# Row maxima over two PSUM banks at once, and one bank for dense outputs and softmax sums

## The reference

```python
xn = group_norm(x)                                   # 32 groups
qkv = einsum('oc,bcn->bon', qkv_w, xn); q, k, v = split(qkv)   # per head
m = softmax(einsum('bct,bcs->bts', q * scale, k * scale), axis=-1)
h = einsum('bts,bcs->bct', m, v)
x = einsum('oc,bcn->bon', proj_w, h) + proj_b + x
```

## Time and profile before

| | us |
|---|---|
| median of 3 runs | 2266.51 (2265.88 to 2267.82) |
| profiled execution, its time | 2263.78 |
| its span, first to last instruction | 2262.0 |
| PE busy | 2193.9 (97%) |
| POOL busy | 1788.2 (79%) |
| DVE busy | 1692.7 (75%) |
| ACT busy | 1274.0 (56%) |

### The profile page before, as it was taken

How to read it: one execution, slowest core, us unless ns; L and a number is a source line. 1 busy time by engine, 2 the same in 40 slices (tenths; PEclk the granted TensorE clock), 3 DMA queues, 4 the chain that set the end, 5 groups by cost and what they waited for, 6 DMA issues and landing times.

```text
span 2262.0 us, 41861 instructions
## 1 busy us (share of the span) xinstructions
PE 2193.9 (97%) x10552; PEld 1091.3 (48%) x10552; DVE 1692.7 (75%) x2896; ACT 1274.0 (56%) x2321; POOL 1788.2 (79%) x567
## 2 busy tenths in 40 slices
PE   5799999999999999999999999999999999999998
PEld 3355454545545455454544545445454544545442
DVE  3677787777877778777777878768777777877772
ACT  2355656566565555656555565655656556565554
POOL 2388878888887978878887888878878788788785
PEclk8799999999999999999999999999999999999999
DMA  4222233322333322233322333222333322433210
GB/s 118 57 69 49 53 95 76 95 43 56 72 75 96 68 68 53 57 95 94 89 40 63 81 76 94 62 61 55 71 94 76 79 45 51 93 76 76 52 43 20
DMA packets 208771, 157.53 MB, mean 70 GB/s; under 512 B 166528, under 2 KB 166784, under 8 KB 208512
## 3 DMA queue, kind: packets, MB, share of 16 engines
q1 hardware_dynamic: 208512, 154.48, 29.8%
HBM read 36.39 MB, written 16.78 MB: 24 GB/s over the span
## 4 chain that ended last, share of the span: by engine, by line
PE 89%; DVE 4%; issue 3%; SPq 1%; ACT 1%; DMA 1%; DVEq 1%; POOL 0%; ACTq 0%; POOLq 0%
PE ps_t L365 25%; PE ps_v L400 21%; PE ps_m L382 19%; PE ps_d L421 9%; PE ps_a L413 5%; PE ps_d L436 5%; PE ps_d L429 5%; SPq L254 1%; DVE raw_max L656 1%; DVE stage_ql L673 1%; DVE att L717 1%; ACT pt L582 1%; DVE rden L707 0%; DMA qs<-neg_max 0%; PE ps_m L421 0%
## 5 line engine op out<-in xcount | busy, mean ns | idle before, releaser
L656 DVE TENSOR_REDUCE raw_max<-ps_m 128x1 f32<-128x512 f32 x2048 | 1332.4, 684 | 444.1 <-PE ps_m L382 413.4
L582 ACT ACTIVATE pt<-ps_t 128x512 f32<-128x512 f32 x2048 | 1141.8, 596 | 919.3 <-PE ps_t L365 913.0
L828 POOL TENSOR_TENSOR acc<-acc,pt 128x2048 f32<-128x2048 f32 x317 | 1448.8, 4570 | 89.5 <-ACT pt L582 61.5
L382 PE MATMUL ps_m<-ks,qs 96*128 96x512 f32 x2048 | 988.0, 483 | 9.0 <-DVE raw_max L656 8.0
L365 PE MATMUL ps_t<-qs,ks 97*128 97x512 f32 x2048 | 879.0, 430 | 30.3 <-issue 13.1
L365 PEld LDWEIGHTS ps_t<-qs,ks 97*128 97x128 f32 x2048 | 389.6, 191 | 656.4 <-ACT pt L582 366.9
L828 POOL TENSOR_TENSOR acc<-pt 128x2048 f32<-128x2048 f32 x64 | 291.8, 4560 | 327.0 <-ACT pt L582 327.0
L400 PE MATMUL ps_v<-pt,v 128*32 128x512 f32 x4096 | 546.5, 606 | 0.0
L382 PEld LDWEIGHTS ps_m<-ks,qs 96*128 96x128 f32 x2048 | 393.0, 192 | 152.2 <-issue 62.7
L421 PE MATMUL ps_d<-xn,wq 128*128 128x512 f32 x500 | 262.7, 608 | 8.2 <-ACT xn L614 5.7
L400 PEld LDWEIGHTS ps_v<-pt,v 128*32 128x32 f32 x4096 | 80.7, 108 | 185.1 <-ACT pt L582 115.1
(11 more groups left out here) (46 smaller groups left out, 531.9 us busy)
## 6 DMA issues: line engine op xcount, KB each, us to landing
ks<-stage_kh SPq DMA_DIRECT2D x256, 128.0 KB, 2.5
qs<-stage_qh SPq DMA_DIRECT2D x256, 128.0 KB, 2.5
ks<-stage_kl SPq DMA_DIRECT2D x128, 128.0 KB, 2.5
qs<-stage_ql SPq DMA_DIRECT2D x128, 128.0 KB, 2.5
qs<-neg_max SPq DMA_DIRECT2D x1024, 0.5 KB, 2.0
xn<-x_dram SPq DMA_DIRECT2D x16, 512.0 KB, 4.0
res<-x_dram SPq DMA_DIRECT2D x16, 512.0 KB, 4.2
between<-res SPq DMA_DIRECT2D x32, 256.0 KB, 2.1
```

The lines of the kernel that those rows point to most:

```text
L382: pe.matmul(ps_m[max_bank(u)][:, :], qs[b][0:KROWS, h, c:c + P], ks[b][0:KROWS, h, kf * HALF:(kf + 1) * HALF], start=True, stop=True).then ...
L582: act.activation(pt[t % 4][:, h, :], ps_t[u % 2][:, :], ACT.Exp, scale=SCALE).then_inc(exp_done, 1)
L656: dve.tensor_reduce(raw_max[:, e % 2, t, kf:kf + 1], ps_m[max_bank(u)][:, :], AX.X, ALU.max)\
L828: pool.tensor_tensor(acc[hf][:, :, :], a[:, :, :], pt[t % 4][:, :, :], ALU.add).then_inc(pool_added, 1)
```

## The change

- The scores for the maxima go in pairs to two double banks `ps_m` of 1024 values. DVE waits for the second of a pair and takes the maximum over both banks by one negating instruction straight into `neg_max`. `raw_max`, the joining instruction (L664) and the semaphore `neg_done` are gone. PE waits for `max_done` once a pair.
- That takes four banks, so `ps_d` and `ps_a` become one bank `ps_x`. The order of its users in a half is new: output 0 (units 0 and 2), the sums (unit 7) and their divide, output 1 (11 and 13), output 2 (17 and 19), output 3 (23 and 25). Each waits for the readers of the one before. Group statistics move to unit 61, their additions to 50, ACT's normalisation to units 11, 15, 19, 23, and POOL's scale and shift behind its last addition.
- SP issues the row of head 3 before the next slot's staging, and interleaves that staging with rows as in later slots.

```diff
-DENSE_AT = 1
-SUMS_AT = 10
+DENSE_AT = ((0, 2), (11, 13), (17, 19), (23, 25))
+SUMS_AT = 7
 DIVIDE_AT = (1, 2, 2, 3)
-GN_AT = 51
-NORMALISE_AT = (13, 17, 25, 29)
+ADD_QUARTERS_AT = 50
+GN_AT = 61
+NORMALISE_AT = (11, 15, 19, 23)
...
-        ps_m = [bank(f"ps_m{b}") for b in range(MAX_BANKS)]
+        ps_m = [ctx.enter_context(nc.psum_tensor(f"ps_m{b}", [P, NH, HALF], F32)) for b in range(2)]
         ps_v = bank("ps_v")
-        ps_d = bank("ps_d")
-        ps_a = bank("ps_a")
+        ps_x = bank("ps_x")
...
-            for e in range(HG - 1):
+            for e in range(HG):
                 load_row(e, 0, e)
-            for h in range(HG):
-                stage_head(1, 1, h)
-            load_row(HG - 1, 0, HG - 1)
-            for u in range(ROWS_AT, UNITS, MAX_GROUP):
-                slot_row(plain(0), u)
...
+            def output_taken(s, hf, r, first, has_second):
+                if hf == 1 and has_second:
+                    pe.wait_ge(qkl_done, 4 * (s.n + 2) + r + 1)
+                elif hf == 0 and s.g == 0 and not first:
+                    pe.wait_ge(proj_done, 4 * (s.j - 1) + r + 1)
+                elif hf == 0 and s.g == 1 and has_second:
+                    pe.wait_ge(v_done, 4 * (s.j + 1) + r + 1)
...
+                if writes and part == 0:
+                    if r > 1:
+                        output_taken(s, hf, r - 1, first, has_second)
+                    elif r == 1:
+                        if not (first and hf == 0):
+                            pe.wait_ge(norm_done, NH * s.n + hf)
...
                     if u == SUMS_AT and not first:
-                        sums(prev, NH - 1, stats_done)
+                        bank_for_sums(s, 0, first, has_second)
+                        sums(prev, NH - 1)
...
-                dve.tensor_reduce(raw_max[:, e % 2, t, kf:kf + 1], ps_m[max_bank(u)][:, :], AX.X, ALU.max)\
-                   .then_inc(max_done, 1)
-                if w % MAX_GROUP == MAX_GROUP - 1:
...
+                dve.tensor_reduce(neg_max[:, e % HG, t:t + 1], ps_m[max_pair(u)][:, :, :].rearrange("p k s -> p (k s)"),
+                                  AX.X, ALU.max, negate=True).then_inc(max_done, 1)
```

More of the change, by code:

```diff
@@ L111, in row_at, with max_pair, dense_at @@
     return NT * slot_n + e
[L114 to L119, removed]
+def max_pair(u):
+    return u // NH % 2
+def dense_at(u, later=0):
+    for r, steps in enumerate(DENSE_AT):
+        if (u - later) % (UNITS // NH) in steps:
+            return r, steps.index((u - later) % (UNITS // NH))
+    return None, None
 def attention_layers(nc, x, w_qkv, w_proj, pars, bias_v, bias_proj, ident_in, group_in, out):
@@ L259, in load_row @@
                 hf, h = e // HG, e % HG
-                sp.wait_ge(neg_done, row + 1)
-                for t in range(NT // NH):
+                sp.wait_ge(max_done, ROW_TILES * (row + 1))
+                for t in range(ROW_TILES):
                     c = hf * HALF + t * P
@@ L332, in _ @@
             turn = B // 2 - 1
+            slot(plain(0))
             body(0, 0, 0)
@@ L376, in scores_for_max @@
                     pe.wait_ge(staged[h], 16 * STAGE_DMAS * (n + 1))
-                back = next(k for k in range(1, UNITS) if max_bank((u - k) % UNITS) == max_bank(u))
-                if not isinstance(n, int) or UNITS * n + w >= back:
-                    pe.wait_ge(max_done, UNITS * n + w - back + 1)
+                pair = UNITS // NH * n + w // NH
+                if kf == 0 and not (isinstance(pair, int) and pair < 2):
+                    pe.wait_ge(max_done, pair - 1)
                 c = hf * HALF + t * P
-                pe.matmul(ps_m[max_bank(u)][:, :], qs[b][0:KROWS, h, c:c + P],
-                          ks[b][0:KROWS, h, kf * HALF:(kf + 1) * HALF],
-                          start=True, stop=True).then_inc(sm_ready, 1)
+                mm = pe.matmul(ps_m[max_pair(u)][:, kf, :], qs[b][0:KROWS, h, c:c + P],
+                               ks[b][0:KROWS, h, kf * HALF:(kf + 1) * HALF], start=True, stop=True)
+                if kf == NH - 1:
+                    mm.then_inc(sm_ready, 1)
             def weighted_values(s, hf, t):
@@ L439, in project_out, with group_stats @@
                     mm.then_inc(proj_ready, 1)
-            def group_stats(j, nsums):
+            def group_stats(j):
                 pe.wait_ge(mv_summed, j + 1)
-                aux_free(nsums)
-                mm = pe.matmul(ps_a[:, 0:2 * CT], group[:, :], channel_mv[:, :, :], start=True, stop=True)
+                mm = pe.matmul(ps_x[:, 0:2 * CT], group[:, :], channel_mv[:, :, :], start=True, stop=True)
                 mm.then_inc(gm_ready, 1)
-            def dense(s, u, first, has_next, has_second):
[L450 to L473, removed]
-                    if part == 0:
[L475 to L486, removed]
@@ L499, in slot @@
-                stats_done = s.j + 2 if s.g == 0 and not first and has_third else None
                 for u in range(UNITS):
                     scores_t(s, u)
-                    if u % HG == DENSE_AT:
-                        dense(s, u, first, has_next, has_second)
+                    dense(s, u, first, has_next, has_second)
                     if has_next or AHEAD + u < UNITS:
```

143 lines of the change are left out of this document (79 added, 64 removed).

## The result

The changed kernel takes 2556.36 us (median of 4, 2549.49 to 2565.85) against 2266.2 before: the ratio is 1.128, 95% interval 1.1245 to 1.1321. The forecast was 2496 with a range of 2440 to 2540. The direction was right, the time lies above the range: 290 us were lost where 230 were forecast. The profiled execution has a span of 2552.5 and a mean granted clock of 0.959, against 0.986.

The account below looks back on a forecast made before the run. PE's own work, busy 97%, was taken to bound the kernel before. Terms 155 + 65 + 46 - 19 - 10 - 12 + 5 = +230 on 2263.8 gave 2494, stated as 2496 for the median; range 2440 to 2540.

Parts of the forecast that it names:

- rival 3: The clock: if each of the 60 waits brought PE's clock down, 240 us more, 2736 in all; chance 0.05.
- Term A: PE's dense matmul of output 1 in unit 11 waits for the divide after unit 7's sums: 2.59 us a half, +155.
- Terms B and C: Runs of four units without dense work, where PE waits for ACT: +65 us; ACT's other copies within such runs: +46.
- C's first part: ACT's raw output copy in unit 4 delays PE in units 4 to 7 of all 60 halves: +29 us.
- The gains: Sums beside a values product -19 us, PE's wait for a queries output gone -10, head 3's row earlier at the start -12.
- Rival 1: At unit 11 the divide in effect overtakes the wide maximum, so only the run's 0.36 counts: 2363 us; chance 0.05.
- Rival 2: PE's own work still sets the end, decided at unit 11; only the gains are left, 2225 us; chance 0.05.

Follow-up runs that it names:

- the first experiment: The changed kernel with all four steps of the divide in unit 8 of DVE's list, ahead of the wide maximum of units 8 and 9: 2349.3 us.

## Why the prediction was wrong, and where it was right

**The step that failed is rival 3, the clock, and the reading of the earlier trace rows that set it aside.** The text said that at the loop edges PE is idle 2.3 "and the stretch of such an edge has 1.00, the 2.4 GHz level", and gave the rival 0.05, outside the range. There are six such edges, and I had looked at one. Busy time by stretch of the kernel before, the first 4 us behind each of the six:

```profile
420.30:424.30 4.00, 4.00 (x21) 2.40 (x21) 2.24 (x4) 2.17 (x4) 0.46 (x1) 1.00 0.48 108
691.90:695.90 4.00, 4.00 (x11) 3.25 (x12) 1.40 (x3) 1.53 (x3) 0.53 (x1) 0.61 0.69 156
964.90:968.90 4.00, 4.00 (x11) 3.22 (x12) 1.50 (x3) 1.63 (x3) 0.77 (x1) 0.61 0.54 121
1238.20:1242.20 4.00, 4.00 (x11) 3.15 (x12) 1.38 (x2) 1.51 (x3) 0.42 (x1) 0.58 0.47 104
1511.30:1515.30 4.00, 3.97 (x11) 3.16 (x12) 1.33 (x2) 1.40 (x3) 0.70 (x1) 0.58 0.48 109
1784.40:1788.40 4.00, 3.96 (x11) 3.15 (x12) 1.32 (x2) 1.39 (x3) 0.66 (x1) 0.58 0.52 115
```

At five of the six the clock fell. The count behind PE's busy time says the same: 11 matmul records where 21 fit. The trace of before thus had the answer: idle times of this length bring the clock down more often than not, and the fall costs about 1.6 us (eight units take 9.46 to 9.48 where it fell and 7.90 where it did not), the most frequent price later too. As an estimate from these rows, five sixths of 60 times 1.6 is 80 us, which would have made the forecast 2576. The sum had no term for the clock; the falls behind these waits measured 71 us. The price in the rival, 4 us a fall from slot 0, was too high as well, 2.1 was measured. So neither "no falls" nor "all waits, 4 us each" held. The rule named there, from the Trainium skill (TensorE: Matmul & The Clock Gate, "A second HAM failure mode: psum-queue depth-cycling"), lays the oscillation on frequent short idles; the first experiment, in which the score matmuls sat idle 102 times for ACT, up to 0.5 us each, has a clock of 0.989, and the only falls of its steady slots, five, are at loop edges. Here it took the longer idle times; whether short idles would do it if they came more often, no run here shows.

**Term A** was right in its mechanism and nearly in its size: 2.59 forecast, 2.52 measured. Units 8 to 11 take 6.45 where four units with a dense matmul need 3.93. Of this 2.26 is the wait (10.38 against 8.12) and 0.26 the run that was counted into it.

**Terms B and C** were right in sum. Without the clock's 71 the profiled loss is 219, forecast 230. The order alone gives 109; the forecast's terms for it, with the run of units 8 to 11 that term A held, are 65 + 22 + 46 - 19 - 10 = 104. C's first part measured 32 for 29. A single run costs less than forecast, 0.26 for 0.36: units 28 to 31 of the first half of an even slot of the changed kernel take 3.33, where 3.07 is work alone.

```profile
885.86 0.50 PE L358 MATMUL ps_t<-qs,ks 97*128 97x512 f32 x1
...
889.19 0.51 PE L358 MATMUL ps_t<-qs,ks 97*128 97x512 f32 x1
```

The 0.36 came from slot 0, where one such run follows another. In the other halves the last four units take 3.46 to 3.68; why was not taken apart.

**The gains** were there: 13 measured for 12 forecast at the start, and for the sums and the wait of unit 49 the two terms, forecast 19 and 10, measured 21 and 10, less the 13 of a new wait in the kernel in which they were tried. They were hidden under the losses.

**Rival 1** is what the first experiment made of the kernel: 2349.3, where the rival had 2363. **Rival 2** falls by the runs: with the divide out of the way the changed kernel is still 3.8% slower.

**The signs named beforehand.** 123 us behind `att` against the 60 that would have refuted term A, 7.5 us more in slot 11 (75.05 against 67.5), and 1024 maxima of 1.222: these came. Two did not. The clock did not stay at 1.00 from slot 1 on, and it had not done so before either. And the view of waits does not show the score matmuls waiting 80 to 110 us more for ACT: their weight loads wait 360.4 us against 366.9 before, the matmuls 29.1 against 3.4. What the runs cost shows in the distances between the starts, not in this view.

**Why a change that frees the vector engine loses 13%.** DVE was not what PE waited for. The wide maximum needs a fourth bank, that bank is taken from the one between the dense outputs and the sums, and the two then need each other's readers to be done. The wide maximum also does its harm by its place: it is ready late and stands ahead of the divide that PE now waits for.

## What to carry to other kernels

When two users are put into one bank, write down the chain from the first one's last write to the second one's first write, with everything that stands in between in the readers' lists, and compare it with the work that the writer has left: here 5.55 us, against the 3.15 that PE's own work was forecast to take, decided it, and moving three short instructions ahead of one long one gave back 207 of 290 us. Where PE and ACT hand two banks back and forth, spread the other matmuls evenly between the scores: a run of four scores without one cost 0.26 to 0.36 us here, and a copy that ACT does within the run another 0.5 to 0.6. Price a new idle time of TensorE of 1 us and more with the clock, and read *all* places of before with such an idle time, not one.

## What the runs showed of the hardware that was not expected

- The clock fell behind waits much shorter than the 12.45 us of slot 0: behind 3 of 60 at 0.94 us, 31 or 43 of 60 at 1.7, 58 of 60 at 2.12, and behind 5 of 6 loop edges at 2.3.
- A fall is not the same each time in one program: 20 of the 34 cost about 1.6 us and 14 about 2.9. The four runs of this kernel spread over 16 us, those of before over 3 beside it and over 9 in another set; that the falls are the cause is likely, since the slower runs have the lower clock (0.954 at 2565.85, 0.961 at 2549.49), but was not tested.
- A maximum over 1024 values in two adjoining banks takes 1.222 us, 0.146 less than two of 0.684; two narrow ones give 1.22 by their slope alone, so crossing the bank's edge costs nothing that shows.
